# Token deviations and q/k norms of the first three attention halves computed apart, in an attention and layers kernel

## What is computed

```
h = layernorm(x) * (1 + ca) + sa                  # modulated by the conditioning rows
xn = layernorm(h, ln_gamma, ln_beta)
q, k, v = xn @ w_q.T, xn @ w_k.T, xn @ w_v.T      # 4 heads of 64
q, k = rmsnorm(q) * q_gamma / 8, rmsnorm(k) * k_gamma
x = x + ga * (softmax(q @ k.T) @ v @ w_o.T + b_o)
h = layernorm(x) * (1 + cb) + sb
```

## Time and profile before

| what | value |
|---|---|
| median of 3 runs | 2089.75 us (2089.67 to 2093.92) |
| the profiled execution, its own time | 2088.22 us |
| its span | 2086.4 us |
| PE, DVE, ACT, POOL busy | 89%, 72%, 57%, 48% |
| projections of half 0 begin | 36.21 us |
| of half 1 | 58.45 us |
| of half 2 | 80.57 us |
| first row maximum on DVE | 98.12 us |

### The profile page before, as it was taken

One profiled execution on the slowest core, in us unless ns is written; L12 is line 12 of the kernel. 1 busy time (PEld: TensorE's weight loads), 2 busy tenths in 40 slices (PEclk: granted clock), 3 DMA queues, 4 the chain that ended last, 5 costly groups with the idle time before them and its releaser, 6 DMA issues.

```text
span 2086.4 us, 36550 instructions
## 1 busy us (share of the span) xinstructions
PE 1859.3 (89%) x12941; PEld 1390.8 (67%) x12941; DVE 1512.6 (72%) x3747; ACT 1185.1 (57%) x2726; POOL 994.1 (48%) x781
## 2 busy tenths in 40 slices
PE   4789999999956999999999998988999999999987
PEld 3644454444424778787787877867787787877776
DVE  6788887777776677686776768777685867768673
ACT  3555556343434665656656566674656656565562
POOL 2234455456655444444444444454545545545361
PEclk7789999999977999999999999999999999999998
DMA  4000000101221000000000002011101000100000
GB/s 159 26 18 28 11 26 23 36 26 63 77 83 44 18 23 13 25 21 18 20 12 23 22 19 66 17 58 32 30 26 30 22 21 27 33 22 27 25 19 23
DMA packets 84615, 68.58 MB, mean 33 GB/s; under 512 B 11029, under 2 KB 79941, under 8 KB 84433
## 3 DMA queue, kind: packets, MB, share of 16 engines
q1 hardware_dynamic: 84433, 66.25, 10.2%
HBM read 45.22 MB, written 16.81 MB: 30 GB/s over the span
## 4 chain that ended last, share of the span: by engine, by line
PE 49%; DVE 29%; ACT 9%; issue 9%; POOL 2%; DMA 1%; DVEq 0%; SPq 0%; ACTq 0%; POOLq 0%
ACT share_x L1485 4%; PE bank_A L102 4%; PE bank_A L104 3%; PE bank_A L103 3%; PE ps_O L484 3%; PE bank_A L1323 3%; PE bank_P L102 3%; PE bank_O L1346 3%; PE bank_T L1334 3%; PE ps_S L457 3%; PE bank_P L104 2%; PE bank_P L103 2%; DVE share_k_lo L1736 2%; DVE mxr L781 2%; DVE share_x L1671 2%
## 5 line engine op out<-in xcount | busy, mean ns | idle before, releaser
L1893 POOL TENSOR_TENSOR share_x<-share_x,l_rinv 128x512 f32<-128x512 f32 (+1 forms) x256 | 251.0, 1002 | 337.3 <-DVE l_rinv L1679 337.0
L1881 POOL TENSOR_TENSOR l_t<-share_qk,share_v 128x512 f32<-128x512 f32 x128 | 179.2, 1421 | 378.5 <-DVE l_ss L1638 375.8
L1485 ACT ACTIVATE share_x<-share_x,l_nb 128x256 f32<-128x256 f32 (+1 forms) x512 | 248.1, 486 | 80.4 <-DVE l_nb L1671 80.1
L102 PE MATMUL bank_A<-share_q_hi,l_w_hi 128*114 128x256 f32 (+1 forms) x768 | 221.3, 288 | 3.2 <-DVE share_q_lo L1716 1.8
L104 PE MATMUL bank_A<-share_q_hi,l_w_lo 128*114 128x256 f32 (+1 forms) x768 | 216.7, 282 | 0.0
L103 PE MATMUL bank_A<-share_q_lo,l_w_hi 128*114 128x256 f32 (+1 forms) x768 | 216.4, 282 | 0.0
L1671 DVE CUSTOM_DVE_ANT_0 share_x<-bank_A,share_scr 128x256 f32<-128x256 f32 (+1 forms) x512 | 177.2, 401 | 37.5 <-PE bank_A L1323 37.3
L584 ACT ACTIVATE pr<-ps_S 128x1024 f32<-128x1024 f32 x128 | 130.8, 1023 | 124.4 <-PE ps_S L460 123.5
L1334 PE MATMUL bank_T<-ident,share_x 128*128 128x128 f32 x960 | 149.3, 286 | 47.2 <-POOL share_x L1893 36.5
L947 POOL TENSOR_TENSOR acc<-acc,pr 128x1024 f32<-128x1024 f32 x64 | 158.2, 2472 | 45.9 <-ACT pr L584 41.3
L781 DVE TENSOR_REDUCE mxr<-ps_M 128x2 f32<-128x1024 f32 x128 | 154.9, 1210 | 34.4 <-PE ps_M L471 33.5
(11 more groups left out here) (282 smaller groups left out, 5101.0 us busy)
## 6 DMA issues: line engine op xcount, KB each, us to landing
share_v<-x_layers SPq DMA_DIRECT2D x64, 128.0 KB, 2.5
share_x<-in_x SPq DMA_DIRECT2D x8, 512.0 KB, 3.9
base_rows<-share_x SPq DMA_DIRECT2D x16, 256.0 KB, 2.1
x_layers<-share_x SPq DMA_DIRECT2D x16, 256.0 KB, 2.1
share_v<-x_layers SPq DMA_DIRECT2D x64, 64.0 KB, 2.2
x_layers<-l_yb SPq DMA_DIRECT2D x32, 128.0 KB, 1.8
share_m<-base_rows SPq DMA_DIRECT2D x32, 128.0 KB, 2.6
out<-l_yb SPq DMA_DIRECT2D x32, 128.0 KB, 1.7
```

Source lines behind the costliest of these rows:

```text
L102: pe.matmul(out, a_hi, b_hi, start=(start and k == 0), stop=False)
L1485: eng.activation(row, row, ACT.Exp, bias=nb[:, R % SS, e:e + 1], scale=-1.0, accum_out=rsum[:, R % SS, e:e + 1]).then_inc(ex_ready, 1)
L1881: eng.tensor_tensor(dst[:, :, :, lo:lo + H2], src[:, :, :, hi:hi + H2], table[:, :, 1, lo:lo + H2].unsqueeze(2).to_broadcast([P, 2, LH, H2 ...
L1893: eng.tensor_tensor(row, row, rinv[:, R % SS, :].unsqueeze(2).to_broadcast([P, 2, P * windows(n)]), ALU.mult).then_inc(pn_ready, 1)
```

## The change

For halves n = 0, 1 and 2 (`APART`) the roots are made in two chains. At tick (n, 5) DVE makes the four tiles' statistics of h1 of half n + 1 (before: one tile at each of j = 6 to 9, between the sums of squares) and then runs the chain on 16 columns, `roots(n)`. At j = 10 `roots_qk(n)` runs it on the 32 columns of the sums of squares. `chain_ready` is raised by each. ACT waits for the first of the two only, and makes the xn tiles of half n + 1 at j = 6 to 9, each behind the eviction of that tick, and not at 12 to 15. The transposes of q and k are moved: those of half 0 stand at (1, 4), (1, 10), (1, 11), (1, 12) and those of half 1 at (2, 4) to (2, 7). All later halves are as before.

```diff
+        APART = (0, 1, 2)
...
-            return sum(is_chain(c) for c in range(-2, n + 1))
+            return sum(is_chain(c) + (c in APART) for c in range(-2, n + 1))
+
+        def token_chains(n):
+
+            return chains(n) - (n in APART)
...
-                at = (0, 4, 11, 12) if n % 2 else (10, 11, 12, 13)
+                at = {1: (4, 10, 11, 12), 2: (4, 5, 6, 7)}.get(n, (0, 4, 11, 12) if n % 2 else (10, 11, 12, 13))
...
-                t.wait_ge(chain_ready, chains(c))
+                t.wait_ge(chain_ready, token_chains(c))
...
-                if j >= 12 and 0 <= n + 1 < A_HALVES:
-                    apply(n, 4 + j - 12, x[:, (n + 1) % 3, j - 12, :], xn_ready)
+                a = j - (6 if n in APART else 12)
+                if 0 <= a < 4 and 0 <= n + 1 < A_HALVES:
+                    apply(n, 4 + a, x[:, (n + 1) % 3, a, :], xn_ready)
...
-                if 0 <= c < A_HALVES:
+                if 0 <= c < A_HALVES and c not in APART:
...
+            def roots_qk(c):
+                t.wait_ge(scr_used, 6 * c + 6)
+                link(eng.tensor_scalar(cv[:, 16:48], ss[:, :, :].rearrange("p a g -> p (a g)"), 1.0 / HD, RMS_EPS ** 2, ALU.mult, ALU.max))
+                rsqrt(eng, link, cr[:, c % 2, 16:48], cv[:, 16:48], ct[:, 16:48])
+                eng.sem_inc(chain_ready, 1)
...
+                if j == 5 and n in APART:
+                    h = n + 1
+                    for a in range(4):
+                        t.wait_ge(h1_ready, 4 * h + a + 1)
+                        stats(x[:, h % 3, a, :], 4 + a, a)
+                    roots(n)
...
-                if 6 <= j < 10 and 0 <= n + 1 < A_HALVES:
+                if 6 <= j < 10 and 0 <= n + 1 < A_HALVES and n not in APART:
...
-                if j == 10 and is_chain(n):
+                if j == 10 and n in APART:
+                    roots_qk(n)
+                elif j == 10 and is_chain(n):
                     roots(n)
```

## The result

| | before | changed |
|---|---|---|
| median of 11 runs each | 2089.6 us | 2097.96 us |
| ratio, with its 95% interval | | 1.0047 (1.0035 to 1.0058) |
| span of the profiled execution | 2086.4 us | 2095.1 us |
| projections of half 1 begin (T1) | 58.45 | 60.93 |
| of half 2 (T2) | 80.57 | 85.26 |

The account below looks back on a forecast made before the run. The early part was taken as a chain through all engines, none full; its 4.0 us delay, added to 2088.2, gave 2092.2 profiled, and 1.5 more gave 2093.8 us. Its own range was 2091.5 to 2096.0, the whole range 2086.0 to 2098.0.

Parts of the forecast that it names:

- the price of DVE's norms: DVE's norms of q and k in each half: 0.61 us each, from a row of the earlier timeline.
- The block at j = 5: Four statistics plus the 16-column chain on DVE at tick 5: 4.83 us, 41.25 to 46.08 in half 0.
- The second chain: The 32-column chain on DVE: taken as 2.75 us, between 2.60 and 3.20.
- Half 0: Stage up to the projections of half 1: they start at 58.3 us, 0.15 us gained.
- norms 52.45 to 54.85: Half 0's four norms on DVE, directly behind its second chain: 52.45 to 54.85 us.
- Half 1: Stage to half 2's projections: DVE idles 2.1 us before a low part; they start at 81.0, 0.4 us later than before.
- Half 2: Stage to DVE's first row maximum: DVE idles 3 us; 21.15 us against 17.55, 3.6 more.
- After T3: Behind DVE's first row maximum (T3, 98.12 us before): order stays, so its 4.0 us delay carries to the end.
- The rival with the clock staying down: PE stays at half clock through half 1's projections: 4.2 us on top, 2098.0 us; chance 0.07.
- The sentence on the cheaper chain by the table: By the skill's instruction table the added chain would be some 1.0 us, not 2.6, and the sum about 1.6 smaller.
- The rival that DVE's extra work falls into its idle time: In the three early stages ACT's parts decide instead: minus 4.9 us, 2084.9 us; chance 0.14.
- The working of the queues: Stepping DVE, ACT and PE through halves 0 to 2 in queue order: first row maximum at 102.1, 4.0 us later.

Follow-up runs that it names:

- pool_held: Changed kernel with POOL's modulation of halves 2 and 3 held until DVE's norms of the half before are done; 2094.26 us, ratio 1.0026.
- clock_kept_up: Changed kernel with 15 matmuls of 512 columns added on PE at ticks (3, 0) to (3, 4); 2097.9 us, ratio 1.0038.
- norms_after_tokens: Changed kernel, split for halves 0 and 1 only, their norms behind the next half's tokens, half 0's transposes behind the second chain; 2085.99 us, ratio 0.9993.
- transposes_only: Kernel before the change with only the transposes of q and k moved to their new ticks, one chain a half; 2095.15 us, ratio 1.0029.
- two_halves: Changed kernel with the split for halves 0 and 1 only, half 2 and its transposes as before the change; 2093.05 us, ratio 1.0024.

## Why the prediction was wrong

**The step that failed** is the price of DVE's norms, 0.61 us each with nothing to slow them, in halves 0 and 1. They ran beside POOL's modulation at about 1.1 us each, and without that meeting T3 comes 3.96 us earlier (pool_held).

**Where the 8.7 us of the profiled execution are.** T3 is 8.67 later: 3.96 from the meeting of DVE and POOL (pool_held), 4.7 from the queues. The projections of half 3 add 2.7 at half clock, so the first row sums are 11.35 later. The 2.7 come back further on, through further differences of the clock, so that the whole is 8.7 longer as T3 is; that the two agree to 0.1 us is luck. The twelfth unit, between two row sums, in the kernel before:

```profile
493.11:526.22 33.11, 29.80 (x163) 15.57 (x165) 22.65 (x28) 9.19 (x10) 15.12 (x7) 0.90 0.18 56
```

and in the changed one:

```profile
504.63:535.43 30.80, 27.47 (x163) 14.09 (x165) 22.67 (x28) 9.18 (x10) 15.15 (x7) 1.00 0.20 61
```

It is 2.3 us shorter since the clock didn't fall in it. In the ten profiled executions this unit takes 30.6 to 33.3 us with a clock of 1.00 to 0.90, while the units ahead of it agree within 0.5 us. Whether a version draws the high or low clock there steadily I didn't test; it may be part of why the runs of one kernel lie 5 to 14 us apart, and why 2.8 us gained in clock_kept_up aren't seen in its median.

**Point by point.**
- *The block at j = 5* (4.83 us forecast): its statistics begin at 41.35 and the first sum behind it at 46.25, 4.90 us. Right. *The second chain* (2.75): 104.37 - 101.51 = 2.86 in half 2. Right within its bounds, since the chain is followed by a short wait. In half 0 it is 53.11 - 49.84 = 3.27, above the bound of 3.20, since its last instruction met POOL's first product. (The one chain of the kernel before is 14 records in its timeline, not the 13 instructions named ahead of the prediction; the two chains are 13 and 12.)
- *Half 0:* everything up to the start of the second chain is within 0.2 us, and the norms start 0.66 late. The step that failed is "norms 52.45 to 54.85", with each norm at 0.61 us. I took it from a row in which POOL had nothing to do, and had myself put POOL's modulation from 51.9 to 57.9. Nothing in the working asked whether the two can run at their old speed together. The kernel before's trace had an answer, in a stretch that I didn't use: DVE and POOL in it,

```profile
136.07 1.10 DVE L843 TENSOR_TENSOR share_qk<-share_qk,cr 128x512 f32<-128x512 f32 x1
...
138.23 1.74 DVE L843 TENSOR_TENSOR share_qk<-share_qk,cr 128x512 f32<-128x512 f32 x1
```

```profile
136.77 5.44 POOL L947 TENSOR_TENSOR acc<-acc,pr 128x1024 f32<-128x1024 f32 x2
```

  the same norm takes 1.10 and 1.74 us beside POOL's sums of two SBUF tensors and 0.68 without.
- *Half 1:* DVE's idle 2.1 ahead of the second low part was 1.9; the norms again took 2.2 us more than forecast. *Half 2:* idle 3 us was 3.2; no POOL beside the norms; 21.53 us against 21.15 forecast. Right.
- *After T3:* "the order is as before, I carry the 4.0 us" held for T3 to the projections (15.13 against 15.11), not for the projections, where the clock came up later in this execution.
- *The rival with the clock staying down* gives 2098.0, next to the measured median, by luck: half 1's projections took 7.8 us (60.93 to 68.69), less than the 8.4 before, and the loss at half clock was 2.7 us, in half 3. *The sentence on the cheaper chain by the table* gives 1.6 us less for the sum; that is one half's share, and three halves have an added chain. The traces' 0.17 us for 16 columns rules that table out, and no term of the sum used it. *The rival that DVE's extra work falls into its idle time* was false for this order and true for another: norms_after_tokens reaches T1 at 57.15.

The working of the queues was right in its mechanism and 0.7 us short in its sum; its parts were tested less well than that, since of the waits taken singly transposes_only was forecast 3.8 us too low. The term that was mis-sized is that of the norms, 8 of them at 0.61 and not about 1.1 us, some 4 us, which with the 4.7 us of the queues gives 8.7 and not 4.0.

## What to carry to other kernels

When a change makes two engines overlap that took turns before, look in the old trace for the same instruction beside the same partner, and take its duration from there. When a chain of roots is split so that one part may start early, ask what stands behind the other part on the in-order queue: here the norms stood ahead of the next half's tokens, and moving them behind the tokens, with the transposes behind the second chain, turned a loss of 4.5 us at T3 (two_halves) into a gain of 1.4, part of it by keeping the norms clear of POOL. An eviction moved to an early tick holds up all that follows it on its engine, however idle that engine looks by its share.

## What the hardware showed

- A VectorE product with both inputs in SBUF (128x512, f32) takes 0.68 us alone. Back to back beside GpSimd's products of 128x256 it takes 1.1 on the mean, and 1.10 and 1.74 in the rows beside those of 128x1024; GpSimd's 128x256 products go from 0.73 to between 1.05 and 1.18. A small one (128x32) took 0.61 and not 0.19. Single norms between low parts kept 0.68 us while GpSimd was slowed.
- Low parts read from PSUM with one SBUF input don't change (in the changed kernel 0.74 us at 58.60 beside GpSimd's product, and 0.74 at 60.05 without one). Neither do sums read from SBUF. Those ahead of T3 never ran beside GpSimd, so their even durations say nothing; later in the kernel before one did, and took its usual 0.68 us:

```profile
240.84 0.68 DVE L897 TENSOR_REDUCE ss<-share_scr 128x8 f32<-128x512 f32 x1
```

```profile
239.03 2.37 POOL L947 TENSOR_TENSOR acc<-acc,pr 128x1024 f32<-128x1024 f32 x1 [0.99 <-ACT pr L584]
241.36 2.52 POOL L975 TENSOR_TENSOR xr<-xr,boga 128x512 f32<-128x512 f32 x2
```

- The Trainium skill, "SBUF — State Buffer", section "Who interferes with whom", says that a VectorE instruction with two SBUF inputs contends with a GpSimd instruction that reads SBUF, and that a reduction doesn't; the traces agree (norms 1.1 for 0.68 us, the sum above at 0.68). Read against the forecast's own schedule, that rule would have pointed at the missing term; its size has to come from a trace.
- The clock of TensorE behind an interrupted stretch (clock 0.50 from T3 on) came up 2.5 us after the start of half 3's projections in the kernel before and 12 us after it in the changed one, for the same instructions. With fifteen matmuls added between the row maxima it was at 1.00 through the whole of them.
